# A decoder layer whose turn is reordered: self softmax beside the cross projections, cross softmax beside output, queries and keys

## The reference

```python
x = x + attn(layernorm(x))         # q, k rotated; causal softmax(q k / sqrt(32)) v; Wo; biases on all
x = x + xattn(layernorm(x), ctx)   # q = qdq(x) @ qdq(wq).T + bq, qdq: int8 rounding per token
                                   # k, v = ctx @ wkv.T + bkv; softmax; qdq(o) @ qdq(wp).T + bp
x = x + moe(layernorm(x))          # 64 experts, top 8 per token, at most 128 rows per expert
```

## Time and profile before

| | |
|---|---|
| median of 3 runs | 1879.45 us (1877.4 to 1882.1) |
| profiled execution | 1883.06 us |
| its span | 1880.5 us |
| PE matmul busy | 1713.6 us, 91% of the span |
| DVE busy | 1261.2 us, 67% |
| ACT busy | 912.2 us, 49% |
| POOL busy | 654.5 us, 35% |
| output projection of turn 1 ends | 79.0 us |
| output projection of turn 32 ends | 1391.0 us |
| first expert's matmul | 1451.2 us |

### The profile page before, as it was taken

How to read it: one execution, slowest core, us unless ns; L and a number is a source line. 1 busy time by engine, 2 the same in 40 slices (tenths; PEclk the granted TensorE clock), 3 DMA queues, 4 the chain that set the end, 5 groups by cost and what they waited for, 6 DMA issues and landing times.

```text
span 1880.5 us, 33123 instructions
## 1 busy us (share of the span) xinstructions
PE 1713.6 (91%) x9512; PEld 1204.0 (64%) x9512; DVE 1261.2 (67%) x3328; ACT 912.2 (49%) x2737; POOL 654.5 (35%) x628
## 2 busy tenths in 40 slices
PE   3999999999999999999999999999983977878785
PEld 2667777777767777777767777777752655555554
DVE  7577777777777777777777777777762444444443
ACT  3356655555556655555556655555551333333332
POOL 4113333332323333332233333333223344444445
PEclk9999999999999999999999999999985999998998
DMA  9802222221100001000000001000043799999995
GB/s 364 315 30 93 100 98 93 77 73 57 42 32 27 23 22 36 26 28 22 22 22 22 22 22 33 29 28 22 17 151 106 224 254 255 263 248 250 253 255 78
DMA packets 130497, 194.43 MB, mean 103 GB/s; under 512 B 35397, under 2 KB 68549, under 8 KB 130472
## 3 DMA queue, kind: packets, MB, share of 16 engines
q1 hardware_dynamic: 91560, 156.27, 24.6%
q0 software_dynamic: 38912, 37.87, 9.9%
HBM read 126.61 MB, written 130.29 MB: 137 GB/s over the span
## 4 chain that ended last, share of the span: by engine, by line
PE 68%; DMA 20%; issue 5%; DVE 4%; ACT 1%; POOL 1%; POOLq 0%; SPq 0%; DVEq 0%
PE bank L408 34%; DMA out<-x,slots 19%; PE bank L419 9%; PE bank L436 6%; PE bank L428 5%; PE bank L391 4%; PE bank L414 3%; DVE kbd L1013 2%; PE bank L444 2%; PE bank L571 1%; PE bank L422 1%; PE bank L396 1%; PE bank L498 1%; POOL routed L1245 1%; DMA probsT<-in_oT_w 0%
## 5 line engine op out<-in xcount | busy, mean ns | idle before, releaser
L1245 POOL DMA_INDIRECT routed<-row,slots x256 | 271.2, 1059 | 284.5 <-DVE chosen_before L942 211.0
L691 ACT ACTIVATE probs<-bank,small 128x128 f32<-128x128 f32 x1024 | 321.6, 422 | 45.6 <-DVE small L907 44.8
L1326 POOL DMA_INDIRECT out<-x,slots x128 | 198.7, 1553 | 230.7 <-DMA out<-x,slots 190.9
L1237 POOL TENSOR_TENSOR small<-small,half 128x1 f32<-128x1 f32 x96 | 53.8, 561 | 579.0 <-DVE small L862 579.0
L907 DVE TENSOR_REDUCE small<-bank 128x4 f32<-128x512 f32 x256 | 171.2, 688 | 54.8 <-PE bank L422 47.2
L691 ACT ACTIVATION_READ_ACCUMULATOR probs<-bank,small 128x1 f32 x512 | 152.3, 301 | 0.0
L428 PEld LDWEIGHTS bank<-idf,probs 128*128 128x128 f32 x1024 | 119.2, 141 | 51.2 <-issue 28.0
L419 PE MATMUL bank<-kbd,qT 128*128 128x512 f32 x256 | 135.9, 613 | 6.6 <-DVE kbd L1013 6.6
L428 PE MATMUL bank<-idf,probs 128*128 128x128 f32 x1024 | 138.4, 273 | 2.2 <-DVE probs L1073 1.4
L678 ACT ACTIVATE probsT<-bank 128x512 f32<-128x512 f32 x256 | 137.2, 635 | 3.6
L436 PEld LDWEIGHTS bank<-xv,probsT 128*128 128x128 f32 x1024 | 123.1, 194 | 11.1 <-issue 10.3
(11 more groups left out here) (245 smaller groups left out, 4094.3 us busy)
## 6 DMA issues: line engine op xcount, KB each, us to landing
w_gate_up<-in_w_gate SPq DMA_DIRECT2D x64, 384.0 KB, 4.5
w_gate_up<-in_w_up SPq DMA_DIRECT2D x64, 384.0 KB, 5.2
w_down<-in_w_down SPq DMA_DIRECT2D x64, 384.0 KB, 6.5
routed<-empty_row SPq DMA_DIRECT2D x4, 5120.0 KB, 21.7
x_in<-in_x SPq DMA_DIRECT2D x32, 256.0 KB, 2.8
ctx_sb<-in_ctxT_in SPq DMA_DIRECT2D x32, 256.0 KB, 2.8
x_res<-in_x SPq DMA_DIRECT2D x32, 256.0 KB, 2.6
out<-x SPq DMA_DIRECT2D x32, 256.0 KB, 2.0
```

The source lines that it names most:

```text
L691: last = act.activation(probs[:, g, j * P:(j + 1) * P], bank[:, b, j * P:(j + 1) * P], ACT.Exp, bias=negmax[:, h:h + 1], **({"accum_out": ...
L1245: pool.indirect_dma_start(routed, bass.IndirectOffsetOnAxis(ap=slots[:, k:k + 1], axis=0), row[:, :], None, bounds_check=SLOTS - 1, oob_is ...
L1326: pool.indirect_dma_start(out.rearrange("b p (h c) -> (b p h) c", h=2), bass.IndirectOffsetOnAxis(ap=place_of[k % 2][:, half_:half_ + 1], ...
```

## The change

The first stage gets another turn structure, and some of its work another form.

- A turn now spans three blocks: self attention of `cur`, cross attention of `cur - 1`, second sum, ffn norm and router of `cur - 2`. Turns 4 to 31 are the hardware loop, and after turn 32 there are two more turns.
- First half of the turn: turned q and k, self scores, self softmax, with the cross key, query and value projections, the value projection and the router between. Second half: cross scores, self values weighed, next queries, output projection, next keys, cross softmax, cross output projection.
- Scores are 16 matmuls of 32 rows and 128 columns each, over four row strips and four banks (one head of each strip next to another), in place of four block-diagonal ones of 512 columns. The block-diagonal tiles and their spreading are gone. The four masks are added ahead of the self scores.
- The bias matmul stays only in `xv`, with 128 rows. The query and key biases are rotated and turned once in setup and added by DVE as it takes the turned q and k out of their banks. The cross key bias is added by DVE too. The value bias goes once through the output projection in setup and is added, with the output bias, to `x_res` by POOL every turn; `xp_bias` is added by POOL into a tile of its own (`x1_bias`).
- All four scaled copies of the cross query are ACT's (two were DVE's).
- DVE's second half is first sum, norm, quantising of x, rotation of the next block, both averages, and quantising of the cross output, in that order.

```diff
+BY_SELF = 6
-CROSS_BANK = (0, 4, 3, 1)
-SELF_BANK = (2, 6, 0, 4)
+CROSS_BANK = (3, 5, 0, 7)
+SELF_BANK = (6, 4, 1, 2)
...
-                steps = [(bias_of[:, BIASES.index(name), :], bias_rows[:, :])]
+                steps = [(ones_r[:, :], xv_rows[:, :])] if name == "xv" else []
...
-            def scores(b, g, q, kb, causal_mask, done):
+            def scores(banks, q, keys, masked, done):
+                for i in range(NG):
+                    for j, b in enumerate(banks):
+                        own = slice(j * DH, (j + 1) * DH)
+                        last = pe.matmul(bank[:, b, i * P:(i + 1) * P], q[own, i, :], keys[own, i, :],
+                                         start=not masked, stop=not masked or i == NG - 1)
+                        if i == NG - 1:
+                            last.then_inc(done, 1)
...
```

More of the change, by code:

```diff
@@ L406, in project @@
                 steps += [(lo[:, t, :], w_hi[:, t, :]) for t in range(KT)]
-                for k in range(first, end):
+                for k in range(first, min(end, len(steps))):
                     last = pe.matmul(bank[:, b, :], steps[k][0], steps[k][1], start=(k == 0),
@@ new lines, in body @@
+                if with_self:
+                    until(pe, d_norm, nth(cur, 8, 4))
+                    turn_probs(SELF_BANK[1], 1, p_pT)
+                if with_before:
+                    until(pe, d_ln["ffn"], nth(prev - 1, 7, 7))
+                    if with_self:
+                        until(pe, a_pT, nth(cur, 4, 1))
+                    turn(6, row[:, 0:D], p_x3T)
+                if with_cross:
+                    cross_values(1, prev)
+                if with_before:
+                    until(pe, a_x3T, prev - 1)
+                    for t in range(KT):
+                        last = pe.matmul(bank[:, 6, 0:E], x3T[:, t * P:(t + 1) * P], router_w[:, t, :],
+                                         start=(t == 0), stop=(t == KT - 1))
+                    last.then_inc(p_log, 1)
@@ L519, in body, with cross_weigh @@
                         turn_probs(CROSS_BANK[g], g, p_xpT)
[L520 to L528 removed]
+                def cross_weigh(g):
@@ L563, in body @@
-                if with_cross:
-                    until(pe, d_ln["ffn"], nth(prev, 7, 7))
-                    turn(5, row[:, 0:D], p_x3T)
-                if with_self and not last_x:
-                    end_queries(cur + 1)
-                if with_cross:
-                    until(pe, a_x3T, prev)
-                    for t in range(KT):
-                        last = pe.matmul(bank[:, 0, 0:E], x3T[:, t * P:(t + 1) * P], router_w[:, t, :],
-                                         start=(t == 0), stop=(t == KT - 1))
-                    last.then_inc(p_log, 1)
+                    turn_bf16(7, xo8, p_o8T)
@@ new lines, in body @@
+                if with_cross:
+                    until(act, p_q8T, prev)
+                    if with_before:
+                        until(act, p_xp, prev - 1)
+                    copy(flat(xq8T), bank_bf16(5), a_q8T)
+                self_exp(0)
+                if with_cross:
+                    until(act, p_xk, prev)
+                    copy(xk_sb[:, :], bank[:, 3, :], a_xk)
+                    until(act, p_cq, prev)
+                    act.activation(cq, bank[:, 5, :], ACT.Copy, scale=x_s).then_inc(a_cq, 1)
@@ new lines, in body @@
+                self_exp(1)
+                copy_self_probs(0)
+                if with_cross:
+                    until(act, p_cqT, prev)
+                    if with_before:
+                        until(act, p_xs, nth(prev - 1, 4, 4))
+                    for g in range(NG):
+                        last = act.activation(cqT[:, g, :], bank[:, 0, g * P:(g + 1) * P], ACT.Identity,
+                                              scale=xq_ws[:, g:g + 1], bias=xq_bs[:, g:g + 1])
+                    last.then_inc(a_cqT, 1)
@@ L721, in body @@
+                if with_self:
+                    until(act, p_v, cur)
+                    until(act, p_pv, nth(prev, 4, 4))
+                    copy(v_sb[:, :], bank[:, 7, :], a_v)
+                self_exp(2)
+                copy_self_probs(1)
+                if with_before:
+                    until(act, p_x3T, prev - 1)
+                    copy(x3T[:, :], bank[:, 6, :], a_x3T)
+                self_exp(3)
+                copy_self_probs(2)
                 if with_before:
```

698 lines of the change are left out of this document (347 added, 351 removed).

## The result

| | before | after |
|---|---|---|
| median | 1878.43 us (1872.98 to 1882.1, 4 runs) | 2184.8 us (2172.8 to 2191.26, 4 runs) |
| profiled execution, its span | 1883.06, 1880.5 us | 2172.8, 2171.0 us |

A forecast was written before the change was run, and what follows sets the result against it. PE bounds the kernel before; after, serial DVE chains and waits give 47.4 us a turn, 51.3 with clock losses. 78.96 + 3 + 31 x 51.3 + 60.2 + 16 + 429.3 = 2177.8, forecast 2177 us; range 2015 to 2325.

The forecast's parts named there:

- PE's work, 35.0: One turn: 42.3 us less 0.15 idle, 2.7 for bias matmuls and 4.4 for scores leaves 35.0.
- Strip scores: Twice 16 matmuls a turn: 1.25 us per 16 if row strips overlap, bounds 0.86 and 3.2; 4.4 saved.
- the walk of the first half: Following the four engine queues from turn start to output projection's end; finds four waits, 6.2 us with small ones.
- Second half, 16.7: Behind the output projection: 14.4 us of serial DVE work and semaphore, then 2.25 through PE and ACT.
- first sum and norm: Start of DVE's second half: 4.3 us instead of 4.8, as POOL's long subtraction no longer runs beside it.
- The hole of 5.54: PE's wait in the second half: about 7 us idle, 6 of it in one piece.
- First half, 31.4 at full clock: Turn start to output projection's end: PE's 25.2 us plus 6.2 of waits.
- The waits forecast at 1.2, 2.5, 1.6 and 0.6: First half: DVE through norm 0; ACT emptying bank 7; norm 3 behind router maximum, exponential; three DVE steps for positions.
- The clock, 3.9 a turn: Half speed after the hole costs 2.7 us; a second slow stretch, in about half the turns, 1.2.
- Rival 1: Loop clock stays full or nearly: turn 45.5 to 49 us, span 2057; chance 0.22.
- The tail, +16: After turn 32: last block's cross part starts later, +9 us; its two cross projections, +7; range 8 to 24.
- Setup, +3: Some ten more DVE bias steps (0.6 us each), bias projection 2.9, less old key-block and bias work; 0 to +6.

The follow-up runs named there:

- fill_both: Changed kernel plus unused matmuls on PE, 24 ahead of its wait for the quantised cross output and 9 ahead of the cross value projection; 2089.39 us, ratio 1.1107.
- chain_longer: Changed kernel plus three unused 512-column DVE steps, 1.0 us, ahead of the last step of the cross output's quantising; 2250.12 us, ratio 1.1529 on its chip.
- first_half_longer: Changed kernel plus the same three unused DVE steps ahead of the self maxima, where DVE waited for PE; 2204.15 us, ratio 1.1277 on its chip.
- old_strip_filled: Kernel before with strip matmuls for the cross scores and 8 unused matmuls ahead of PE's turned cross probabilities; 1958.37 us, ratio 1.0011 on its chip.

## Why the prediction was right

- **PE's work, 35.0.** Take the clock's 4.1 and the six waits' 11.8 from 51.2 and 35.3 are left; in fill_both's turns of 47.1 PE is busy 42.8, and without the two fills of 7.45 that is 35.35. Strip scores: next start 1.10 later, forecast 1.25 in this sum and 1.1 in the walk of the first half, lower bound 0.86. The Trainium skill's rule in "TensorE: Matmul & The Clock Gate", LDWEIGHTS, read as one load after another over the strips, would have given 3.2; the rows exclude that.
- **Second half, 16.7.** DVE's chain is 13.8 (14.4 forecast; first sum and norm took 3.8 for 4.3), and from the output projection's end to the next turn's first transposes it is 51.2 - 34.1 = 17.1, part of it at half clock. The hole of 5.54 was forecast as 6. chain_longer beside first_half_longer shows that the chain is the path.
- **First half, 31.4 at full clock.** The waits forecast at 1.2, 2.5, 1.6 and 0.6 were 0.72, 2.23, 1.34 and 0.90. From 866.40 to the output projection's end at 900.53 are 34.1 with the clock in it.
- **The clock, 3.9 a turn.** 4.1. It was mis-split: the second fall comes in every turn, not in half of them, and the stretch is shorter. Rival 1, clock up, would be 47.1 a turn, as fill_both's best turns are; the chip doesn't keep it up.
- **The tail, +16.** +13.8. Turn 32 still ends in a hole of 5.62 before the cross output.
- **Setup, +3: the term that was mis-sized.** It is +13.9, outside its bounds of 0 to 6. The number of DVE's bias steps was about right, but two of them weren't 0.6 long. Timeline of all engines, after, setup first and then two rows of a steady turn:

```profile
27.65 4.90 POOL L1368 TENSOR_TENSOR w_xv_lo<-probs,w_xv_hi 128x2048 fp32r<-128x2048 f32 x1 [3.39 <-ACT w_xv_hi L850]
28.16 4.68 DVE L1195 TENSOR_SCALAR xn<-xn,idf 128x512 f32<-128x512 f32 x1
...
32.52 4.67 POOL L1368 TENSOR_TENSOR w_o_lo<-probsT,w_o_hi 128x2048 fp32r<-128x2048 f32 x1
...
32.87 4.87 DVE L1196 SCALAR_TENSOR_TENSOR xv_rows<-xv_rows,idf,xn 128x512 fp32r<-128x512 f32 x1
...
40.04 0.68 DVE L961 TENSOR_TENSOR xT_lo<-bank,xT_hi 128x512 fp32r<-128x512 f32 x1
...
40.78 1.22 PE L431 MATMUL bank<-w_q_hi,xT_lo 128*128 128x512 f32 x2 [7.83 <-DVE xT_lo L961]
...
883.60 1.27 POOL L1334 TENSOR_TENSOR x_res<-x_res,att_bias 128x512 f32<-128x512 f32 x1
...
883.96 1.45 DVE L1125 TENSOR_TENSOR probs<-probs,small 128x512 f32<-128x512 f32 x1
```

Each of the two DVE steps (28.16 and 32.87) began shortly after a long subtraction of POOL's had begun and ended 0.3 and 0.6 us after its end: 9.55 us for two steps of a size that takes 0.4 to 0.7 elsewhere, so some 8.4 too long. Taken off the 13.9, that leaves about 5.5, inside the forecast's bounds (an estimate from these rows; no experiment moved the steps). The low part of the first x, for which PE waits 7.83, stands in DVE's queue behind all of them: it begins at 40.04, and at 25.77 in the kernel before, 14.3 earlier. Setup before had a stall of the same kind (before, POOL and DVE):

```profile
27.11 4.58 POOL L1300 TENSOR_TENSOR w_o_lo<-probsT,w_o_hi 128x2048 fp32r<-128x2048 f32 x1
28.69 3.02 DVE L1149 TENSOR_SCALAR xq_ws<-rstep 128x4 f32<-128x4 f32 x1
```

That step on four columns takes 0.17 in the changed kernel, where POOL is done by then: 2.9 us came back. The bias projection (forecast 2.9, about 3.0 in the trace) came on top.

The numbers also cancelled: setup was 10.9 too low, and the turns 31 x 0.49 = 15 and the tail 2.2 too high. The good total owes something to that; the mechanism doesn't.

## What to carry to other kernels

Before work is taken off a full engine, find which other chain is nearly as long: here 7 us of PE work went away and 11.8 us of waits came. 6.6 of them (5.54, and 1.09 for ACT's copy behind it) come from a hand-ordered turn that put 13.8 us of dependent DVE steps behind one event; the other 5.2 are the first half's. Count waits at the price of the clock too: a wait of 1.94 us cost another 1.7 in four turns of five. The cheapest test is a fill of unused matmuls in the wait, which adds nothing to the path. What paid in the old order was the plain part, biases folded ahead of the loop.

## What the runs showed of the hardware

- **The clock made less work slower.** 2.3 us less PE work per turn and a wait of 1.94 in its place gave +2.3%. Equal waits ended with the clock up in one turn (42.3) and down in four (44.0). In the changed kernel unused matmuls in two waits gave back 95 of 2185 us. "TensorE: Matmul & The Clock Gate" of the Trainium skill, HAM oscillation, tells of a kernel that restarts slow after a wait in each of its steps; the rows here agree for waits of 5.5 us, and add that one of 1.94 can do, though one of 2.04 in old_strip_filled didn't.
- **DVE stalls beside POOL.** Apart from the two steps in setup it shows in each turn. The same multiplication of probabilities, at 0.69 us in its quiet places, took 1.45 where POOL's addition L1334 had begun 0.36 before it (883.60 and 883.96 above). The prediction took 0.5 off the norm for a stall of this kind, but had no term for it in setup or here; what the 0.76 is worth on the path wasn't measured. The Trainium skill, "SBUF — State Buffer", Who interferes with whom, says that such a pair doesn't share: the one that starts first has the port until its instruction ends. Both places agree: the two steps in setup ended 0.29 and 0.55 behind POOL's, this one 0.54.
- **One chip ran the old order 4% longer.** The kernel before took 1956 us there and 1879 to 1881 elsewhere; the changed order lost 0.9% at most (2204 against 2184.8, with the three steps that took no path). DVE's second average, for instance, idled 1.60 us there for something the trace puts on none of the core's engines (old_strip_filled, DVE):

```profile
729.46 0.21 DVE L924 RECIPROCAL small<-bank 128x8 f32<-128x8 f32 x1 [1.60 <-remote]
```

No trace from the other chips lists such a wait. What it is stays open.
